# A 32-block recurrent layer pipeline on one core: the second feed-forward product and the layernorm move into the following step

## What is computed

```python
x = L0_attn_x                              # (8, 512, 128)
xn = _layernorm(x, axis=-1)
def block(h, p):                           # four layers, each sequence by itself
    k, q, v = split(h @ wkqv, 3)
    r = tril(q @ k.T) / norm               # rows divided by their clipped sum
    r = r @ v
    a, gate = split(r @ w1 + b1, 2)
    m = a * silu(gate) @ w2 + b2
    m = groupnorm1(m, gg, gb)              # mean, variance over a whole sequence
    y = m + h
    f = gelu(y @ wf1 + bf1_) @ wf2 + bf2_
    return layernorm(f + y, lg, lb)
s = block applied four times to xn
g = silu(ffn(xn))                          # each token by its one chosen expert
return x + s * g
```

## Time and profile before

| | |
|---|---|
| median of 3 runs | 515.69 us (514.87 to 517.4) |
| the profiled execution | 514.47 us |
| its span, first to last instruction | 512.4 us |
| PE busy | 475.0 us (93%) |
| DVE busy | 384.8 us (75%) |
| ACT busy | 253.7 us (50%) |
| POOL busy | 252.5 us (49%) |

### The profile page before, as it was taken

The page is one execution under the profiler, slowest core; times in us unless marked ns, Lnnn a source line. Parts: engine busy times, 40 slices in busy tenths (PEclk is TensorE's granted clock), DMA queues, the critical chain, the costliest instruction groups (busy, mean ns, idle before and its releaser), DMA issues.

```text
span 512.4 us, 9849 instructions
## 1 busy us (share of the span) xinstructions
PE 475.0 (93%) x3147; PEld 395.4 (77%) x3147; DVE 384.8 (75%) x1348; ACT 253.7 (50%) x533; POOL 252.5 (49%) x279
## 2 busy tenths in 40 slices
PE   6999889999999999999999999999999999997472
PEld 5887666667888988898889888988888888675242
DVE  4768888878777786677777866777778777888766
ACT  4822434444566655555666555556665544453420
POOL 4520288887545445554454455544444555333341
PEclk9998999999999999999999999999999999999856
DMA  9999411112511111110111111201111000500202
GB/s 265 232 122 222 156 37 38 37 33 78 103 64 58 42 58 42 59 63 32 59 57 44 58 51 48 65 31 59 62 51 46 10 12 12 164 1 1 61 19 84
DMA packets 47345, 35.05 MB, mean 68 GB/s; under 512 B 13320, under 2 KB 38736, under 8 KB 47296
## 3 DMA queue, kind: packets, MB, share of 16 engines
q1 hardware_dynamic: 44496, 28.94, 22.1%
q0 software_dynamic: 2272, 4.71, 2.7%
q10 hardware_dynamic: 528, 0.79, 0.5%
HBM read 14.70 MB, written 9.42 MB: 47 GB/s over the span
## 4 chain that ended last, share of the span: by engine, by line
PE 67%; DVE 12%; POOL 10%; issue 6%; DMA 2%; ACT 2%; POOLq 0%; SPq 0%; DVEq 0%; ACTq 0%
PE bank L1221 9%; PE bank L1148 7%; PE bank L1132 7%; POOL x_slots L471 5%; PE pair L1290 4%; PE pair L1266 4%; PE bank L1303 4%; PE bank L1159 4%; PE pair L1248 4%; PE bank L1160 4%; PE bank L1161 3%; PE pair L1292 3%; PE pair L1246 3%; PE bank L1203 2%; PE bank L1219 2%
## 5 line engine op out<-in xcount | busy, mean ns | idle before, releaser
L483 POOL TENSOR_TENSOR zhat<-zhat,all_lg 128x512 f32<-128x512 f32 x31 | 43.9, 1418 | 88.1 <-PE bank L1193 74.2
L1221 PE MATMUL bank<-all_f,G_sb 128*128 128x128 f32 x512 | 76.8, 284 | 0.0
L651 ACT ACTIVATE y_sb<-bank,gn_bi,gn_sc 128x512 f32<-128x512 f32 x32 | 24.9, 778 | 104.3 <-DVE gn_bi L993 104.2
L1221 PEld LDWEIGHTS bank<-all_f,G_sb 128*128 128x128 f32 x512 | 70.9, 201 | 1.4 <-issue 1.4
L646 ACT ACTIVATE uT_h<-bank 128x512 fp32r<-128x512 f32 x32 | 19.1, 597 | 100.8 <-PE bank L1203 100.8
L426 POOL TENSOR_TENSOR ln_rs<-ln_ve,half_neg 128x4 f32<-128x4 f32 x32 | 33.1, 1033 | 42.0 <-DVE ln_ve L675 41.7
L1132 PEld LDWEIGHTS bank<-moe_w,h_T 128*128 128x128 f32 x312 | 39.5, 191 | 13.9 <-issue 13.9
L498 POOL TENSOR_TENSOR gn_rs<-gn_ve,half_neg 128x1 f32<-128x1 f32 x32 | 18.5, 577 | 58.5 <-DVE gn_ve L888 58.4
L563 ACT ACTIVATE h_T<-bank,w_t 128x128 f32<-128x128 f32 x156 | 44.5, 372 | 5.1 <-PE bank L1148 5.1
L518 POOL DMA_INDIRECT y_rows<-yt,slot_info x39 | 40.9, 1048 | 11.0 <-POOL yt L515 11.0
L631 ACT ACTIVATE G_sb<-bank,all_par 128x512 f32<-128x512 f32 x64 | 43.1, 694 | 5.2 <-PE bank L1184 2.8
(11 more groups left out here) (177 smaller groups left out, 1233.8 us busy)
## 6 DMA issues: line engine op xcount, KB each, us to landing
w_t<-moe_w SPq DMA_DIRECT2D x39, 258.0 KB, 2.4
x_slots<-moe_w SPq DMA_DIRECT2D x1, 2515.5 KB, 20.4
xt<-x_slots SPq DMA_DIRECT2D x39, 64.0 KB, 1.8
x_sb<-in_L_attn_x SPq DMA_DIRECT2D x8, 256.0 KB, 5.7
moe_w<-in_L_ffn_w SPq DMA_DIRECT2D x1, 2048.0 KB, 20.0
moe_w<-y_rows SPq DMA_DIRECT2D x8, 256.0 KB, 4.6
out<-moe_w SPq DMA_DIRECT2D x7, 256.0 KB, 2.4
all_f<-in_L_attn_Wf SPq DMA_DIRECT2D x2, 512.0 KB, 4.2
```

The costliest lines, as they stand in the source:

```text
L483: pool.tensor_tensor(zhat[:, b % 2, :, :], zhat[:, b % 2, :, :], all_lg[:, li, :].unsqueeze(1).broadcast_to([P, C, D]), ALU.mult)\
L1221: last = mm(bank[7][:, at_c], G_sb[:, k, at_c], all_f2[:, li, k, :], start=False, stop=k == 1)
```

## The change

- z (`gelu_second`) is no longer issued at the rear of step s for group s-2, but near the front of step s+1, behind S and q. Its statistics go with it: DVE takes statistics and moments behind the y split, and writes its zhat half behind A_sb and the EARLY xtT copy. zhat's transposition goes from before or behind the first feed-forward product to TensorE's rear, behind the LATE expert product and ahead of `u_by_feature` and `means`.
- y has two buffers. Scale and bias, y_sb and the addition of hT go from the rear of a step to the front of the next.
- All steps 8 to 31 are parted; before, steps 8, 15, 22, 29, 30 and 31 were not.
- On DVE the order is now: scale and bias, S, y, y split, layernorm statistics, EARLY expert addition, gate (919, 929), A_sb (912), EARLY xtT, zhat half, u, w2's statistics, LATE expert addition, groupnorm moments, uT split. The moments stand ahead of the uT split in every step.
- On POOL: scatters of place 0, the layernorm's root, EARLY scaling and DMA, scatters of place 1, htok (written from zhat through itself), the splits of later layers' weights (three in step 7, two ahead of the root before), LATE scaling and DMA, the groupnorm's root, scatters of place 2. In step 2 the two scatters of place 1 are now ahead of the groupnorm's root.
- The output's work is spread otherwise: tanh and silu of two sequences in each of steps 30 to 33, and `outputs` of 1, 2 and 3 sequences in steps 31, 32 and 33, behind the groupnorm moments.
- In the drain TensorE gets products whose result nobody reads: 2 and 3 in step 32, 6 in step 33, 2 in step 34 (`keep_warm`, into bank 5).

```diff
             def step(l, t):                                  # POOL
+                scatter(l, t, 0)
+                if w := at(l, t, 3, B, LB):
+                    ln_pow(w[0], w[1])
+                tile_rows(l, t, EARLY)
+                scatter(l, t, 1)
                 w = at(l, t, 3, B, LB)
...
-                tile_rows(l, t, EARLY)
-                scatter(l, t, 0)
                 if first and t == B - 1:
-                    for k in range(1, L - 1):
+                    for k in range(1, L):
                         split_f1(k)
                 tile_rows(l, t, LATE)
                 if w := at(l, t, 1, B, LB):
                     pool.wait_ge(gn_var, w[0] + 1)
...
-                scatter(l, t, 1)
-                if w := at(l, t, 2, B, LB):
-                    ln_pow(w[0], w[1])
...
+                if w := at(l, t, 2, B, LB):                  # DVE, front
+                    n, b, _ = w
+                    dve.wait_ge(gn_done, n + 1)
+                    dve.tensor_tensor(y_sb[:, n % 2, :], y_sb[:, n % 2, :], hT[:, b, :], ALU.add).then_inc(y_done, 1)
...
+                if w := at(l, t, 3, B, LB):
+                    dve.wait_ge(pe_z, w[0] + 1)
+                    ln_stats(w[0], w[1])
+                    ln_moments(w[0], w[1])
+                tile_out(l, t, EARLY)
...
+                if w := at(l, t, 0, B, LB):                  # DVE, behind 919 and 929
+                    n, b, _ = w
+                    dve.wait_ge(pe_A, n + 1)
...
+                tile_in(l, t, EARLY)
...
+                if w := at(l, t, 3, B, LB):
+                    n, b, _ = w
+                    ln_shifts(n, b)
...
+                if l == L and t == 0:                        # TensorE
+                    pe.wait_ge(yt_done, TILES)
+                if l == L and t == 2:
+                    keep_warm(2, bank[5])
+                gelu_second(l, t)
+                if l == L and t == 1:
+                    keep_warm(6, bank[5])
...
                 tile_back(l, t, LATE)
-                if first:
-                    tile_front(l, t, EARLY, n2 * 2 + 2)
-
-                for stage in ((gelu_second, means, u_by_feature) if first and 2 <= t < B - 1 else
-                              (means, gelu_second) if l == L else (u_by_feature, gelu_second, means)):
-                    stage(l, t)
+                zhat_by_feature(l, t)
+                u_by_feature(l, t)
+                means(l, t)
```

More of the change, by code:

```diff
@@ L103, in retention_moe_kernel @@
         th_sb = sb("th_sb", [P, S])
-        y_sb = sb("y_sb", [P, S])
+        y_sb = sb("y_sb", [P, 2, S])
         G_sb = sb("G_sb", [P, 2, S])
@@ L277, in parted @@
         def parted(l, t):
-            return turn(l, t, EARLY) is not None and l > 0
+            return 0 < l < L
         def parted_steps(l, t):
             return sum(parted(k // B, k % B) for k in range(l * B + t + 1))
-        def halves(l, t):
-            return (0, 1) if parted(l, t) else (1, 0)
         def ring(i):
@@ L589, in late_turn_before @@
             def late_turn_before(l, t):
-                if turn(l, t, EARLY) is not None or l * B + t == 0:
+                if l * B + t == 0:
                     return None
@@ L608, in step @@
                 first = l == 0
-                ends = l == L
-                if not first or t < 2:
-                    queries(l, t)
-                if parted(l, t):
-                    w = at(l, t, 2, B, LB)
-                    act.wait_ge(y_done, w[0] + 1)
-                    act.activation(y_h[:, :], y_sb[:, :], ACT.Copy).then_inc(y_high, 1)
-                if not parted(l, t):
-                    gate(l, t)
-                layernorm(l, t)
-                tile_gelu(late_turn_before(l, t))
-                if parted(l, t):
-                    gate(l, t)
+                tile_gelu(late_turn_before(l, t))
+                if w := at(l, t, 2, B, LB):
+                    n = w[0]
+                    act.wait_ge(gn_affine, n + 1)
+                    act.activation(y_sb[:, n % 2, :], bank[6][:, :], ACT.Identity, bias=gn_bi[:, :],
+                                   scale=gn_sc[:, :]).then_inc(gn_done, 1)
+                queries(l, t)
+                if parted(l, t):
+                    n = l * B + t - 2
+                    act.wait_ge(y_done, n + 1)
+                    act.activation(y_h[:, :], y_sb[:, n % 2, :], ACT.Copy).then_inc(y_high, 1)
+                gate(l, t)
                 if first and t == 1:
@@ L646, in step @@
                     act.activation(uT_h[:, :], bank[2][:, :], ACT.Copy).then_inc(uT_done, 1)
-                if first and 1 <= t < B - 1:
-                    queries(l, t + 1)
-                if w := at(l, t, 1, B, LB):
-                    act.wait_ge(gn_affine, w[0] + 1)
-                    act.activation(y_sb[:, :], bank[6][:, :], ACT.Identity, bias=gn_bi[:, :],
-                                   scale=gn_sc[:, :]).then_inc(gn_done, 1)
-                if turn(l + (t + 1) // B, (t + 1) % B, EARLY) is not None:
-                    tile_gelu(turn(l, t, LATE))
             steps(act, step, L, B, LAG)
@@ L920, in step @@
                         .then_inc(gt_done, 1)
-                if not first:
-                    tile_in(l, t, EARLY)
                 if w := at(l, t, 1, B, LB):
@@ L1078, in logits, with keep_warm @@
                 last.then_inc(pe_gate, 1)
-            def keep_warm(count):
+            def keep_warm(count, dst=bank[6]):
                 for _ in range(count):
-                    mm(bank[6][:, 0:2 * P], ident[:, :], ones[:, :], start=True, stop=True)
+                    mm(dst[:, 0:2 * P], ident[:, :], ones[:, :], start=True, stop=True)
             keep_warm(8)
@@ L1274, in step @@
                     mm(bank[5][:, TE:2 * TE], ones[:, 0:P], oh, start=True, stop=True).then_inc(pe_prefix, 1)
-                if not first:
-                    tile_front(l, t, EARLY, n2 * 2)
-                if parted(l, t):
-                    zhat_by_feature(l, t)
+                tile_front(l, t, EARLY, n2 * 2)
                 gelu_first(l, t, 0)
                 gelu_first(l, t, 1)
-                if not parted(l, t):
-                    zhat_by_feature(l, t)
+                if l == L and t == 0:
+                    keep_warm(2, bank[5])
                 if w := at(l, t, 0, B, LB):
```

139 lines of the change are left out of this document (59 added, 80 removed).

## The result

The changed kernel takes 561.8 us (median of 4 runs, 560.8 to 564.3), the kernel before, run beside it, 515.3: 1.091 times the time, interval 1.085 to 1.097. The forecast was 541 with a range of 521 to 550: right in direction, 21 us short, and outside the range.

What follows compares the result with a forecast made beforehand. TensorE bound steps 8 to 27 before; now a chain through the root would. Span 512.4 + 11.9 (first layer) + 11.1 (full steps) + 2.3 (short) + 2.0 (last) - 1.2 (drain) = 538.5; forecast 541 us, range 521 to 550.

Steps and rivals of the forecast that it cites:

- Link 2: Full step: the groupnorm's root stands behind POOL's LATE scaling and DMA, beginning at U+5.05, a gain of 0.37 us.
- The full step: Full steps with two expert turns: 15.46 us against 14.81, 0.65 more in each of 17, +11.1 us.
- the ring: Full step: the chain from U (end of u) through root, y, gate and xtT copy back to U, summed to 15.46 us.
- Short steps: Steps 15 and 22: u waits for A_sb, 14.3 us from U to U against 13.17, +2.3 in both.
- Parting saves 0.3 a step: The six newly parted steps save 0.3 us of TensorE each, hidden in waits.
- The first layer: First layer, bound by POOL: htok waits for zhat, root to root 14.5 in three steps; +11.9 us in all.
- Steps 1 to 3: Start of the first layer: A_sb behind the gate, two scatters ahead of the root, waiting for the layernorm root; +3.8 us.
- Step 7: First layer: three splits and htok stand ahead of the root; root to root 15.3 against 12.57 us, +2.7.
- Steps 28 to 31: Last steps before the drain: 14.5, 14.3, 13.1 and 13.1, 55.0 us against 52.97, +2.0.
- The drain: After the last steps: y comes 2.8 us earlier, but DVE's outputs and last preparation stand ahead of the last statistics; -1.2 us.
- The one at 560 us: Rival: the root on POOL blocks the gate (919), up to 1.0 us in each of 19 steps; chance 0.06.
- The others: Rivals: TensorE stays the bound, 508, chance 0.09; full steps keep their time, other parts lose, 530 or 524, chance 0.20.

Runs made afterwards that it cites:

- e5_no_idle: The changed kernel without the four groups of idle products in the drain, all else as in the change: 562.3 us, ratio 1.093.
- e62_loads_root: The changed kernel with TensorE's register loads behind S and q and GpSimd's groupnorm root ahead of the LATE scaling and DMA: 550.3 us, ratio 1.068.
- the unparted kernel: The changed kernel with steps 8, 15, 22, 29, 30 and 31 not parted, as in the kernel before: 558.7 us, ratio 1.082.
- the mended kernel: The changed kernel with register loads later, groupnorm root ahead of the LATE scaling, scatters placed otherwise and six steps unparted: 542.6 us, ratio 1.049.
- e8_mended_mask: The mended kernel with A_sb and the EARLY xtT copy ahead of both halves of the gate on VectorE: 548.0 us, ratio 1.062.
- b3_idle_before: The kernel before with idle products between the chain's products of the drain (9, 3, 2, 6 and 2), nothing else changed: 513.2 us, ratio 0.994.
- b1_all_parted: The kernel before with steps 8, 15, 22, 29, 30 and 31 parted too, nothing else changed: 534.7 us, ratio 1.035.

## Why the prediction was right in direction and short in size

- **The bound moves from TensorE to the chain behind the root: right in part.** The changed kernel's full step has the waits that the forecast named: root behind GpSimd's DMA, y split behind y_h (both within 0.1 of their place), the half product behind xtT (0.7 late). Link 2 (the root behind the LATE DMA) was drawn rightly but does not bind: with it gone the step stayed at 15.61. What the chain passes through instead is TensorE's own back product.
- **The full step, the term that failed.** Forecast were 0.65 a step and 11.1 us in the 17; measured are 24.6. That is 13.5 of the 23.7 us by which the span missed 538.5. The step of the argument that failed was the list of what TensorE does between U and its back product: the prediction counted the products and took it that "the change adds no products there", and not the two register loads in its queue, which cost nothing in the order of before (ratio 1.000 when moved). With the loads later the step is 15.62 and 10 us are gone. The other 0.16 a step is about what the LATE front product waits for the LATE addition (0.2), a link that the sum did not have. The sum had the EARLY addition follow the moments, which it does not: it waits for TensorE. That the ring closed near the right number without the loads rests in part on this luck.
- **Short steps 14.3: right** (14.24 and 14.25), by the mechanism given: u waits for A_sb, by 0.60 in step 15.
- **Parting saves 0.3 a step: wrong** as a price. In the order of before it costs 17 us in six steps, part of it the clock's, in the new about 0.5 a step. It did not show in the sum because the forecast had put it under cover.
- **The first layer: right mechanism, wrong size.** 11.9 forecast, 18.3 measured. Steps 1 to 3 came out at +4.3 (3.8) and step 8 from root to root at 14.4 (14.3). The cycles between were taken at 14.5, the middle between a free statistic (14.0) and one held beside htok (15.0); the hold happened in each (a statistic of 0.87 to 1.21 us), and they took 15.7, 15.2 and 15.5. Those are 2.8 us of the miss; even the held price, 15.0, would have been 1.3 short. Step 7 took 18.5 and not 15.3: TensorE ran at the lower of its two clocks, 1.2 GHz, from 124.1 to 130.9 (granted 0.51, after 16 us in which it had been busy for 12.1), and four products of z took 1.06 instead of 0.61. In the profile without the idle products (e5_no_idle), whose code is the same up to the drain, the clock stays up there and the cycle is 15.55; it is low one step earlier instead (granted 0.75 from 108 to 112, 0.82 from 112 to 116), where the layernorm's root stands behind six scatters anyway, and that cycle still takes 15.49. In the profile of e62_loads_root it falls in step 7 again, and the cycle is 18.4. So these 3 us come and go with the execution. They may be why the profiled one lies 2.5 us above the median; the other executions have no trace that could tell.
- **Steps 28 to 31: 57.3, forecast 55.0.** Steps 29 and 30 came as forecast (14.26 and 13.18 for 14.3 and 13.1). Step 28 took 15.66 for 14.5, of which the loads are 0.6, and step 31 14.24 for 13.1: parting it costs 1.1, as the unparted kernel shows.
- **The drain: forecast -1.2, measured +0.4.** That idle products hold the clock up and that this changes nothing in the changed kernel are both shown (1.093 without them, 1.091 with them).
- **The rivals.** The one at 560 us hit the number and not the mechanism: the gate's first half took 0.68 at 342.06 in after, beside a layernorm's root that began at 341.24. The others would have been nearer to 515 than the forecast, in the wrong direction. The range left out what was not on the list at all; it was built from errors in the links and not from links that were missing.

By the Trainium skill ("SBUF — State Buffer", section "SBUF: two separate sides") a VectorE operation with two SBUF inputs and a GpSimd operation that reads SBUF exclude each other. The rows agree for htok: 1.21 for 0.22, and where htok was moved, the small operations beside it took 1.15 and 1.23 and ended with htok's. They do not agree for the layernorm's root of 128x4, beside which 512-wide operations with two such inputs kept their 0.68 and 0.69.

The Trainium skill ("Runtime: NRT & Kernel Launch", section "Instruction fetch mechanics") gives a register load about 200 ns per register. The row here says 299, with 151 for the register work behind it, and the measured one decides: with the page's figure in place of the row's the two would end at about 335.0 (an estimate, 335.2 less twice 0.1), just with the products queued ahead of S, and the gap would not have been seen.

**What stays open.** That the ring of the full step still holds the mended kernel at 15.6 is read from the waits in the trace; the run that took a part of VectorE's work out of it (e8_mended_mask) made another link late and does not prove it. The remaining 11.9 us of the first layer in the mended kernel were not separated further. That step 7 fell to the lower clock in this execution and not in others was seen and not brought about on purpose.

## What to carry to other kernels

When products are moved away from a place in an engine's queue, look at what else stands there: register loads cost nothing as long as work is queued ahead of them (517.2 against 516.9 here), and half of their 1.2 us a step once it isn't (11 us in all). A new order has to be costed as a ring: follow every engine until the ring closes, and ask at each link which of two inputs comes last, since shortening one of them (the root by 1.2 us) may change nothing, and swapping two (A_sb and the gate) only hands the wait to the next engine. A small helper that is priced at a gain of 0.3 us (parted products) can cost ten times that in another order: run it alone first.

## What the runs showed of the hardware that was not expected

- A register load from SBUF on TensorE's queue takes 295 to 495 ns (median 299 of 39), with 151 ns of register work behind it. Two of them exposed cost 0.6 us a step.
- VectorE operations on 128x1 take 0.87 to 1.27 us instead of 0.15 to 0.22 beside htok on GpSimd, whichever operation it is that falls there (958 or 961 before; 973 or 976 after; 888 and 893 with htok moved), and end within 0.03 us of htok's operation. The one between 888 and 893 (890) keeps its 0.15: it lies over the 0.08 us between htok's two operations.
- TensorE's granted clock was 0.70 in the drain without idle products, in either kernel, 0.86 with the change's and 0.89 with the more of b3_idle_before, and in the one kernel where z lay on the chain this gave 2.4 us of span (512.4 to 510.0).
- The same waits (0.4 and 1.63 us) ahead of the same products were followed by the higher clock in step 15 of b1_all_parted and by the lower one in step 22 (granted 0.69 from 341.90 to 347.36), which made the step 1.6 us longer.
